# Two layers of attention and gated FFN on one core: block 1 of the FFN joins the blocks of seven products, with work moved between GpSimd, VectorE and ScalarE

## The reference

```python
x = x + attn_a(layernorm(x))     # 16 heads of 32, causal, qkv = x @ W_qkv.T + b
x = x + ffn(layernorm(x))
x = x + attn_b(layernorm(x))     # the same form, other weights
x = x + ffn(layernorm(x))        # the same FFN weights
# ffn: gate = x @ w_gate.T; up = x @ w_up.T; (silu(gate) * up) @ w_down.T, hidden size 2048
```

## Time and profile before

| | us |
|---|---|
| median of 3 runs (1983.52 to 1985.54) | 1983.87 |
| the profiled execution, its own time | 1981.08 |
| its span, first to last instruction | 1979.4 |
| TensorE busy | 1954.9 |
| VectorE busy | 1159.8 |
| GpSimd busy | 982.2 |
| ScalarE busy | 805.8 |

### The profile page before, as it was taken

One profiled execution on the slowest core, in us unless ns is written; L12 is line 12 of the kernel. 1 busy time (PEld: TensorE's weight loads), 2 busy tenths in 40 slices (PEclk: granted clock), 3 DMA queues, 4 the chain that ended last, 5 costly groups with the idle time before them and its releaser, 6 DMA issues.

```text
span 1979.4 us, 27849 instructions
## 1 busy us (share of the span) xinstructions
PE 1954.9 (99%) x10288; PEld 1442.3 (73%) x10288; DVE 1159.8 (59%) x2387; ACT 805.8 (41%) x1478; POOL 982.2 (50%) x767
## 2 busy tenths in 40 slices
PE   7999999999999999999999999999999999999999
PEld 6655588888866568888885656888888565688887
DVE  5777455445677745544567774445457777544544
ACT  2487522221258752222116774322221686432221
POOL 5314469763230436976433053797534215289740
PEclk9999999999999999999999999999999999999999
DMA  5333111121333311311253331121113333012111
GB/s 161 95 88 76 34 43 54 54 64 43 85 87 76 76 44 32 107 53 54 75 139 87 76 76 44 36 62 53 53 43 86 87 80 82 24 43 64 54 43 43
DMA packets 58821, 132.37 MB, mean 67 GB/s; under 512 B 10560, under 2 KB 11584, under 8 KB 58688
## 3 DMA queue, kind: packets, MB, share of 16 engines
q1 hardware_dynamic: 58688, 130.60, 24.2%
HBM read 75.51 MB, written 4.19 MB: 40 GB/s over the span
## 4 chain that ended last, share of the span: by engine, by line
PE 94%; ACT 2%; DVE 2%; DMA 1%; SPq 1%; issue 1%; POOL 0%; ACTq 0%; DVEq 0%; POOLq 0%
PE bank L1354 11%; PE bank L1356 11%; PE bank L1355 11%; PE bank L1488 11%; PE ring L1354 11%; PE ring L1355 11%; PE ring L1356 11%; PE bank L1461 8%; PE ring L1430 7%; PE ring L1345 1%; ACT prob L861 1%; SPq L555 1%; DMA area<-kq_parts 1%; ACT kq_parts L844 0%; ACT area L940 0%
## 5 line engine op out<-in xcount | busy, mean ns | idle before, releaser
L861 ACT ACTIVATE prob<-bank 128x512 f32<-128x512 f32 (+1 forms) x512 | 273.1, 570 | 158.5 <-PE bank L1461 133.0
L655 POOL TENSOR_SCALAR area<-w_stage 128x1024 fp32r<-128x1024 f32 x126 | 144.3, 1146 | 374.2 <-PE bank L1356 190.0
L657 POOL TENSOR_TENSOR area<-w_stage,area 128x1024 fp32r<-128x1024 f32 x126 | 302.0, 2397 | 10.5
L1168 DVE TENSOR_TENSOR x<-x,bank 128x512 f32<-128x512 f32 x256 | 170.4, 684 | 232.2 <-PE bank L1356 231.6
L732 POOL TENSOR_SCALAR_AFFINE_SELECT prob<-prob 128x512 f32<-128x512 f32 x128 | 82.7, 647 | 446.5 <-ACT prob L861 356.1
L1098 DVE CUSTOM_DVE_ANT_0 xn<-ring,mask_row 128x384 bf16<-128x384 f32 (+7 forms) x384 | 244.2, 663 | 66.8 <-PE ring L1430 65.3
L1354 PE MATMUL ring<-xt_hi,area 128*128 128x512 f32 x672 | 263.7, 392 | 1.3 <-DVE area L1201 1.3
L1355 PE MATMUL ring<-xt_lo,area 128*128 128x512 f32 x672 | 262.0, 390 | 0.0
L1356 PE MATMUL ring<-xt_hi,area 128*128 128x512 f32 x672 | 261.8, 390 | 0.0
L1461 PE MATMUL bank<-area 98*128 98x512 f32 (+3 forms) x768 | 244.7, 374 | 2.6 <-ACT prob L861 1.4
L1461 PEld LDWEIGHTS bank<-area 98*128 98x128 f32 x768 | 133.1, 188 | 125.1 <-ACT prob L861 83.6
(11 more groups left out here) (172 smaller groups left out, 3612.5 us busy)
## 6 DMA issues: line engine op xcount, KB each, us to landing
w_stage<-ffn_w SPq DMA_DIRECT2D x96, 512.0 KB, 3.5
area<-kq_parts SPq DMA_DIRECT2D x336, 128.0 KB, 2.4
w_stage<-attn_w SPq DMA_DIRECT2D x32, 512.0 KB, 4.3
area<-attn SPq DMA_DIRECT2D x48, 128.0 KB, 4.0
x<-x_in SPq DMA_DIRECT2D x16, 256.0 KB, 3.9
out<-x SPq DMA_DIRECT2D x16, 256.0 KB, 2.0
bias_rows<-row_bias SPq DMA_DIRECT2D x8, 256.0 KB, 3.9
masked<-x_in SPq DMA_DIRECT2D x4, 256.0 KB, 4.2
```

What stands on the lines that cost most here:

```text
L655: pool.tensor_scalar(hi, src, 1.0, 0.0, ALU.mult, ALU.add).then_inc(w_hi_done, 1)
L657: pool.tensor_tensor(lo, src, hi.bitcast(F32), ALU.subtract).then_inc(w_split, 1)
L861: act.activation(prob[:, step % PROB_BUFS, h, off:], scores_at(u, j, h), ACT.Exp, scale=SCALE).then_inc(prob_ready, 1)
L1168: dve.tensor_tensor(x[:, t, :], x[:, t, :], row_bank(s, n)[:, :], ALU.add).then_inc(rows_drained, 1)
```

## The change

1. `QUAD_FIRST` becomes 1: FFN block 1 is computed by seven products too. Slots 11 and 12 (block 1's gate and up) get block sums and are now split within `POOL_ORDER`; loads up to slot 13 stand in `SP_ORDER`. The differences stay before slot 13, but they now serve block 1.
2. The first of the six difference operations (x22 - x12) moves from GpSimd to VectorE, behind the last transposed tokens' low part.
3. The high parts of slots 13 and 14 and of the first block sums of block 2 are made by ScalarE. `diff_to_hi` and `diff_to_lo` are placed anew.
4. At the start, each x tile has a semaphore of its own; variance, power and normalisation go by pairs of tiles; VectorE makes the low parts of the first two weight slots. The rows of ones are set in three pieces, one by VectorE at the very start, two by GpSimd (3072 elements each) before and behind the first powers.
5. All five order strings are new, with the same counts, but for two w more in `POOL_ORDER` and two l more in `SP_ORDER`.

```diff
-QUAD_FIRST, QUAD_LAST = 2, BLOCKS - 2
+QUAD_FIRST, QUAD_LAST = 1, BLOCKS - 2
+CAST_BY_ACT = (FFN_SLOT0 + 5, FFN_SLOT0 + 6)
+SPLITS_BEFORE, LOADS_BEFORE = FFN_SLOT0 + 5, FFN_SLOT0 + 6
+FIRST_ONES = 3072
 ORDER = (
...
-    "ssvvvssfssvssvssvssffssvssvssfssfssvvvvvssfssssfssssvvvv",
+    "ssvvssfssvssvssvssffssfssfssvvvssvssfssfssssvvvvssssvvv",
 ACT_ORDER = (
...
-    "eeoeeeeeeeeeeeeeeeeeeeeeeeeexeox",
+    "eeoeeeeeeeeeeeeeeeeeeeeeeeeeexox",
 POOL_ORDER = (
-    "bbdwbwwmmmbbmwbmbmmmmmmmmmmmmmmmawaawammammmmwmmabamdmmmwd",
+    "dwbmwmmbmwbmmmbmmmbmmmmmmwbmmmmbwaabmammmamammamwadmmwmmwwdw",
@@ gpsimd, split_weights
+                if j in CAST_BY_ACT:
+                    low_part(it, n, j)
+                    return
@@ gpsimd, s_split
-                pool.wait_ge(s_step, s_steps(it, b, w, 3))
-                pool.tensor_scalar(both[:, 0, :, :], sums, 1.0, 0.0, ALU.mult, ALU.add
-                                   ).then_inc(s_step, 1)
+                if (b, w) != (QUAD_FIRST + 1, 0):
+                    pool.wait_ge(s_step, s_steps(it, b, w, 3))
+                    pool.tensor_scalar(both[:, 0, :, :], sums, 1.0, 0.0, ALU.mult, ALU.add
+                                       ).then_inc(s_step, 1)
@@ gpsimd, start
-            pool.memset(k_stack[3 * HEAD:3 * HEAD + 2, 1:, :, :].bitcast(F32), 1.0).then_inc(ones_ready, 1)
-            pool.wait_ge(ones_ready, 1)
-            inverse_deviation(0, 0, 0)
+            pool.memset(ones_rows[:, 0:FIRST_ONES], 1.0).then_inc(const_ready, 1)
+            pool.wait_ge(const_ready, CONSTS + 1)
+            for r in range(2):
+                pool.wait_ge(var_ready, r + 1)
+                t = slice(2 * r, 2 * r + 2)
+                pool.tensor_tensor(rstd[:, t], var_eps[:, t], minus_half[:, 0:2], ALU.pow).then_inc(rstd_ready, 1)
+            pool.wait_ge(rstd_ready, 2)
             pool.wait_ge(xn_ready, CT)
...
+            pool.memset(ones_rows[:, FIRST_ONES:], 1.0).then_inc(ones_ready, 1)
@@ scalar
-                for s in range(1, QUAD_STEPS[0]):
-                    for t in range(BT):
-                        silus(s, t)
-                        hidden_hi(s, t)
-                        if s in (1, 2):
-                            diff_to_hi((s - 1) * BT + t)
+                silus(1, 0)
+                hidden_hi(1, 0)
+                diff_to_hi(0)
+                diff_to_hi(1)
+                silus(1, 1)
+                hidden_hi(1, 1)
+                diff_to_hi(2)
+                weights_to_hi(CAST_BY_ACT[0])
+                weights_to_hi(CAST_BY_ACT[1])
+                diff_to_hi(3)
                 for b in range(QUAD_FIRST, QUAD_LAST + 1):
                     for m in KEPT:
                         for w in range(2):
                             keep(b, m, w)
+                        if b == QUAD_FIRST:
+                            beside_kept(m)
@@ scalar, new
+                def weights_to_hi(j):
+                    act.wait_ge(w_split, it * SLOTS + CAST_BY_ACT[0])
+                    act.wait_ge(w_loaded[j % 2], (it * (SLOTS // 2) + j // 2 + 1) * 16)
+                    act.wait_ge(ring_full, full(it, ("gu", 1, BT - 1)))
+                    act.activation(w_part(j, slice(0, SLOT))[0], w_stage[:, j % 2, :], ACT.Copy).then_inc(w_hi_done, 1)
+                def sums_to_hi(b, w):      # called by beside_kept("m6")
+                    act.wait_ge(s_step, s_steps(it, b, w, 3))
+                    act.activation(s_parts(b, w)[:, 0, :, :], s_sums(b, w), ACT.Copy).then_inc(s_step, 1)
@@ vector
+                first_difference()
                 add_rows(0)
-                for s in range(1, QUAD_STEPS[0]):
-                    for t in range(BT):
-                        hidden_parts(s, t)
-                        if s in DIFF_STEPS:
-                            diff_to_lo(BT * DIFF_STEPS.index(s) + t)
-                    for d in downs_after(s):
-                        add_rows(d)
+                hidden_parts(1, 0)
+                diff_to_lo(0)
+                hidden_product(1, 1)
+                diff_to_lo(1)
+                hidden_lo(1, 1)
+                diff_to_lo(2)
@@ vector, quad_block
-                    add_rows(2 * b - 1)
+                    add_rows(2 * b - 1, range(2))
+                    if b == QUAD_FIRST:
+                        diff_to_lo(3)
+                    add_rows(2 * b - 1, range(2, CT))
@@ vector, start
-            chunk_stats(0, 0)
-            normalise_pair(0, 0, 0)
-            normalise_pair(0, 0, 1)
+            for t in range(CT):
+                dve.wait_ge(x_loaded[t], 16)
+                tile_stats(t, x[:, t, :])
+                if t % 2:
+                    variances(t + 1, range(t - 1, t + 1))
+            first_normalise(0)
+            first_weights_lo(0)
+            first_normalise(1)
             xt_to_lo(0, 0, 0)
+            first_weights_lo(1)
             xt_to_lo(0, 0, 1)
```

More of the change, by code:

```diff
@@ L224 @@
+    "ereroeexerxeererrerexee",
+    "exeeeeeeoeeeerererererereereeereexrexeeerer",
+    "erreeoeereerereeeex",
+    "eeoeexeeeeeeeeeeeeeeeeeeeeeeee",
+    "eeeeoeeeeeeee",
+    "eeoeeeeeeeeeeeeeeeeeeeeeeeeeexox",
 )
 DVE_ORDER = (
[L228 to L230 removed]
+    "nnmnnnmnmnmmmmmmmqmmmqmmqmmqmmmmmqqmmmmmqmmmmmmmqmmmmmmmmmmmmmmmmqmmmqmmmmmmmmrmmrrrmmmrmmrmmrrmrrmrrmmm"
@@ L327, in block_kernel @@
         out_bank, den_bank = bank[2], bank[3]
-        x_loaded = [sem(f"x_loaded{c}") for c in range(CHUNKS)]
+        x_loaded = [sem(f"x_loaded{t}") for t in range(TT)]
         x_staged = [sem(f"x_staged{c}") for c in range(CHUNKS)]
@@ L585, in _ @@
                     maxima = iter(range(UNITS))
-                    loads = iter(range(AHEAD, FFN_SLOT0 + 4))
+                    loads = iter(range(AHEAD, LOADS_BEFORE))
                     for what in "".join(SP_ORDER):
@@ L597, in _ @@
                         load_biases(1 - layer)
-                    for i in range(FFN_SLOT0 + 4, SLOTS + (AHEAD if it < LAST else 0)):
+                    for i in range(LOADS_BEFORE, SLOTS + (AHEAD if it < LAST else 0)):
                         if i == STAGE_BEFORE and it < LAST and first_layer(it + 1):
@@ L701, in diff_sum @@
                     (t4, early_hi[:, 2:4, :], t2, ALU.subtract, 4),
-                    (t4, t4, early_lo[:, 2:4, :], ALU.add, 5))[n]
-                if step:
-                    pool.wait_ge(diff_step, it * 6 + step)
+                    (t4, t4, early_lo[:, 2:4, :], ALU.add, 5))[n - 1]
+                pool.wait_ge(diff_step, it * 6 + step)
                 pool.tensor_tensor(dst, a, b, op).then_inc(diff_step, 1)
@@ L740, in add_out_bias @@
                     if first_layer(it):
-                        pool.wait_ge(x_loaded[t // CT], (it // LAYERS + 1) * (16 * CT))
+                        for n in range(t, t + CT):
+                            pool.wait_ge(x_loaded[n], (it // LAYERS + 1) * 16)
                     pool.wait_ge(xn_ready, it * 2 * TT + t + CT)
@@ L799, in iteration @@
                 pool.wait_ge(xn_ready, it * 2 * TT + 2 * TT)
-                for i in range(FFN_SLOT0 + 3, SLOTS + (2 if it < LAST else 0)):
+                for i in range(SPLITS_BEFORE, SLOTS + (2 if it < LAST else 0)):
                     if i == DIFFS_AT:
                         pool.wait_ge(ring_drained, drained(it, ("ln2", 3)))
-                        for n in range(6):
+                        for n in range(1, 6):
                             diff_sum(it, n)
@@ L1007, in _ @@
         def _(dve):
+            dve.memset(k_stack[3 * HEAD:3 * HEAD + 2, 0, :, :].bitcast(F32), 1.0).then_inc(ones_ready, 1)
             dve.memset(ones[:, :], 1.0).then_inc(ring_drained, RING_CREDIT)
@@ L1017, in chunk_variance, with variances, first_normalise, first_weights_lo @@
                 n = it * 2 * TT + ln * TT + (c + 1) * CT
-                dve.wait_ge(stats_done, 2 * n - CT)
-                for t in range(c * CT, (c + 1) * CT):
+                variances(n, range(c * CT, (c + 1) * CT))
+            def variances(n, tiles):
+                dve.wait_ge(stats_done, 2 * n - len(tiles))
+                for t in tiles:
                     dve.bn_aggr(mean_var[:, t, :], stats[:, t, :]).then_inc(stats_done, 1)
                 dve.wait_ge(stats_done, 2 * n)
-                t = slice(c * CT, (c + 1) * CT)
+                t = slice(tiles[0], tiles[-1] + 1)
                 dve.tensor_scalar(var_eps[:, t], mean_var[:, t, 1], EPS, None, ALU.add).then_inc(var_ready, 1)
+            def first_normalise(r):
+                dve.wait_ge(rstd_ready, r + 1)
+                for t in (2 * r, 2 * r + 1):
+                    dve.tensor_scalar(xn_tile(t), x[:, t, :], mean_var[:, t, 0:1], rstd[:, t:t + 1],
+                                      ALU.subtract, ALU.mult).then_inc(xn_ready, 1)
+            def first_weights_lo(i):
+                hi, lo = w_part(i, slice(0, SLOT))
+                dve.wait_ge(w_hi_done, i + 1)
+                dve.tensor_tensor(lo, w_stage[:, i, :], hi.bitcast(F32), ALU.subtract).then_inc(w_split, 1)
```

(4 more changed lines are left out.)

95 lines of the change are left out of this document (50 added, 45 removed).

## The result

| | before | changed | ratio, 95% interval |
|---|---|---|---|
| median of the runs, us | 1983.87 | 1966.32 (1965.85 to 1969.31) | 0.9911 [0.9897, 0.9926] |
| profiled execution, us | 1981.08 | 1965.85 | |
| its span, us | 1979.35 | 1964.12 | |

I had forecast 1978.6 us and a range of 1967 to 1986. The start and the two stops came out near their forecasts. The step that failed was the order strings, which I had priced at nothing.

The account below looks back on a forecast made before the run. The kernel was taken as bound by the number of TensorE instructions. The sum 3.1 + 4 x (3.05 - 0.2 - 1.9 - 0.4) = 5.3 us took 1983.87 to 1978.6 us, range 1967 to 1986.

Parts of the forecast that it names:

- The start: Program start: first 128x512 matmul at 13.5 us instead of 16.67, 3.1 us earlier, bounds 2.0 and 4.0 us.
- the two stops: TensorE waits in the second FFN: 0.2 us at product m6 of block 1, 1.9 us at block 2's m1.
- the order strings: Other moves in the engines' order strings: taken as 0 us an iteration, between -1.5 and +1.5 us.
- the end of the attention: Unit 7's last masks, with slot 9 put between them: 0.4 us net loss an iteration, between -1 and +3.5.
- The ten slow matmuls: First matmuls at 0.44 us each, 16.67 to 21.07 us: up to four could become fast, 0.9 us, not summed.
- The 12 matmuls: FFN block 1 as seven products: 84 matmuls instead of 96, saving 2.72 us in each of four iterations.
- the switch: FFN change from plain steps to products: TensorE's wait for VectorE's row additions goes, 0.33 us gained an iteration.
- The three collisions: VectorE low-part subtractions among GpSimd's differences: three of 1.09 us each, 3.3 us in all, delaying GpSimd.
- no lock: Alternative for VectorE and GpSimd's shared SBUF port: if they only overlapped, collisions cost nothing, block 2's stop 0 us.
- Slot 12: GpSimd before the FFN differences: this slot with sums ends about 761.2 us, 3.6 us of cover, costing nothing.
- rival D: Attention masks: slot 9's 3.5 us stand fully before the last values each iteration, 7.1 us slower, 1991; 12%.
- Rival B: Second FFN and attention: the stops aren't there and the tail is even, 15.3 us gained, 1968.6; 25%.

Follow-up runs that it names:

- late stack: Changed kernel with six more 64 KB DMAs to a scratch array on SyncE's queue before unit 3's stacking DMAs in each iteration; 1983.56 us, ratio 0.9999.
- transposes: Changed kernel with 24 identity transposes before TensorE's first wait, 1966.34 us; with ScalarE's casts for slot 15 as well, 1958.89 us.
- taking the collisions away: Changed kernel without the low parts of the first three differences (VectorE subtracts 8 of 512 columns); 1964.41 us, ratio 0.9905.

## Why the prediction was wrong

**The step that failed is the order strings**, "I take 0 for them, between -1.5 and +1.5 us", with "0.4 us of net loss an iteration" for the end of the attention. Forecast for both: -1.6 us. In the traces attention and projections gain 6.1 us. The strings alone gain 5.9 us by the profiles and 9.6 us by the medians, or 1.5 and 2.4 us an iteration. The first of these is at the edge of my bounds and the second outside. The reason that I gave for 0 and for the bounds is what was wrong: I took TensorE at 99% for full, and half of its idle time, 3.1 us an iteration, for all that an order can win or lose. The strings leave the idle time as it was (24.5 and 25.1 us) and take 6.6 us off the busy time of the same instructions. Over their pitch the matmuls of the kernel before lose 131.3 us, and only 8.7 us of that, behind the first wait, is idle.

My first account of the gain, that ScalarE holds up fewer weight loads, does not stand either: behind a group of weighed values the delay is the same under any name, and of the loads elsewhere only 2.2 us are gained. Where in the order the other 3.7 us lie stays open. No run changed one kind of neighbour and nothing else.

**The ten slow matmuls.** The sum takes 0, the working 0.9 us at most. They were worth 2.1 us between the two traces, but this is not owed to the change: with the start undone they are absent as well. The Trainium skill, "TensorE: Matmul & The Clock Gate", section "What's actually happening", ties the rise to activity. That the transposes of the new start spare it slow matmuls is not what the executions show: 0 to 11 slow ones with the old start, 0 to 8 with the new one. The same section also says that the number of slow matmuls differs between runs of one kernel; had I taken that sentence with the other, the term would have been a spread and no gain, and the runs agree with it.

**The clock in the attention** was in no step. By the medians the strings gain 9.6 us, by profiles without a fall 5.9. The difference is the clock, by the mean granted clock of each run. Of the 40 runs of the kernel before beside the experiments 10 have 1.000, with a median of 1981.7 us; the other 30 have 0.996 to 0.999 and a median of 1985.1 us. All four runs of the strings alone have 1.000 (1975.4 us), and so have all 23 runs with all new strings, late stack and transposes aside. At 1.000 the strings gain 6.3 us; the other 3.4 are falls of the clock in the kernel before. Why the new strings have fewer falls is not shown, only likely: three of four profiles with the old TensorE string have them, in a unit 3 at or behind waits of 0.9 to 1.9 us for a stacking DMA, and no profile with all new strings has such a wait in a unit 3. The late stack made waits and had falls. But waits as long also passed without a fall.

**What was right.** The 12 matmuls and the switch with both stops: 0.95 us an iteration forecast, 0.79 to 0.88 measured; 0.23 for 0.2 us at m6, 1.86 for 1.9 us at block 2, and GpSimd's low part of slot 15 ends there. The start: 2.9 us by its own experiment for 3.1. It is 3.8 us at the first matmul and, against the old start, 4.4 us at the first row scores, so some of it is lost again behind them. The three collisions of 0.9 us each were there. But with "no lock" the second stop would not have gone "from 1.9 to 0 us", as the working says: taking the collisions away was worth 0.7 us a time at both stops together, as ScalarE's casts are late right behind them. Slot 12 had 4.5 us of cover for 3.6. Slot 9 between the masks (rival D) stopped nothing, as argued against it, but with 0.2 us to spare.

By medians, of 17.5 us: the strings 9.6, the start 2.9, and block 1, as what remains, 5.0, in which the luck of the clock's rise counts as well; four FFNs gain 3.3. The parts lean on one another: put into the kernel before the strings are worth 9.6 us, taken out of the changed kernel 15.3. With the old strings block 1 is worth some 0.5 us.

Rival B gave 1968.6 us, nearest to the time, for a reason that wasn't there: both stops stand. A right number would have been a coincidence.

## What to carry to other kernels

TensorE at 99% is not TensorE at its pitch: compare its busy time for the same number of instructions, and price a matmul by the distance of starts. A name beside an idle time is not yet its cause: look at the same place where another name stands, as with the 0.84 us above. An order string is judged with the others as a set; half a set was worse than none. When a stop is left on one engine while another idles in the same stretch, as GpSimd and ScalarE before block 2, moving two casts is a cheap next gain: it made 1959.12 us, a ratio of 0.9874 to the kernel before.

## What the runs showed of the hardware

- At or behind single waits of 0.93 to 3.21 us of TensorE in the attention, the granted clock fell to 0.50 for 3.4 to 13.7 us; that costs half of the length. In the two such stretches that are shown, TensorE was some 80% busy before the fall. Other waits there, of 1.1 to 2.2 us, brought none, nor did the 24 stops of 1.6 us at block 2 in six profiles.
- The full pitch came after 0 to 11 slow matmuls in executions of kernels with the same, old start.
- The first matmul of scores or maxima behind a group of weighed values (128x512) started 0.52 to 0.54 us after the group's last one, in each of 228 places of two traces, while a group behind a group followed after 0.41 to 0.43 us. The idle time of its weight load, 0.84 us, was put down to whichever semaphore came last.
- A plain normalisation on VectorE collides with GpSimd as a two-input operation does. Timeline of VectorE in the changed kernel, beside GpSimd's sums:

```profile
741.37 1.76 DVE L1111 TENSOR_SCALAR xn<-x,mean_var,rstd 128x512 f32<-128x512 f32 x2 [1.21 <-POOL rstd L737]
```

The pair takes 1.00 us at 7.28 us, and 1.76 here, though this operation reads one tile and two columns of scalars.
